# PSUM places of one bank, a fourth score bank, and the attended rows handed to ScalarE and GpSimd in an attention stage on Trainium2

## The reference, cut to what matters

```
def _L1_xattn_ref(q, k, v):              # q: normed x (4, 512, 512); k = v = ctx (4, 512, 128)
    qh = q.reshape(B, S, 8, 4, 16).transpose(0, 2, 3, 1, 4)
    kh = k.reshape(B, S, 8, 16).transpose(0, 2, 1, 3)
    vh = v.reshape(B, S, 8, 16).transpose(0, 2, 1, 3)
    scores = einsum('bkgsd,bktd->bkgst', qh, kh) / sqrt(16)
    weights = softmax(scores)
    out = einsum('bkgst,bktd->bkgsd', weights, vh)
    return out.transpose(0, 3, 1, 2, 4).reshape(B, S, E)
x = x + _L1_xattn_ref(_layernorm(x), ctx_512, ctx_512)
```

## Time and profile before

| what | value |
|---|---|
| median of three runs | 1669.87 us (1669.15 to 1671.94) |
| the profiled execution, its span | 1670.3 us |
| TensorE busy | 1567.2 us, 94% |
| VectorE busy | 948.0 us, 57% |
| ScalarE busy | 717.6 us, 43% |
| GpSimd busy | 702.1 us, 42% |

### The profile page before, as it was taken

The page is one execution under the profiler, slowest core; times in us unless marked ns, Lnnn a source line. Parts: engine busy times, 40 slices in busy tenths (PEclk is TensorE's granted clock), DMA queues, the critical chain, the costliest instruction groups (busy, mean ns, idle before and its releaser), DMA issues.

```text
span 1670.3 us, 24439 instructions
## 1 busy us (share of the span) xinstructions
PE 1567.2 (94%) x8124; PEld 1047.5 (63%) x8150; DVE 948.0 (57%) x1539; ACT 717.6 (43%) x1160; POOL 702.1 (42%) x479
## 2 busy tenths in 40 slices
PE   6869999999889999999899899999999999999998
PEld 4555657565543434434333778788788888788886
DVE  6998979796878897887885622222122222222221
ACT  5885646455547777777677211111111111111111
POOL 1124251633513125254354765670862180930064
PEclk9889999999898999999999999999999999999999
DMA  9189800000231445243430625231440140530088
GB/s 357 56 305 386 291 1 1 0 1 1 84 94 47 123 132 149 82 126 111 148 114 28 224 70 189 82 120 32 182 176 26 59 155 26 188 127 26 26 140 213
DMA packets 90944, 196.16 MB, mean 117 GB/s; under 512 B 7153, under 2 KB 9074, under 8 KB 90226
## 3 DMA queue, kind: packets, MB, share of 16 engines
q1 hardware_dynamic: 71746, 156.68, 28.2%
q0 software_dynamic: 7168, 17.04, 4.5%
q10 hardware_dynamic: 11952, 21.43, 3.9%
HBM read 113.28 MB, written 81.32 MB: 117 GB/s over the span
## 4 chain that ended last, share of the span: by engine, by line
PE 68%; DVE 16%; POOL 6%; ACT 4%; issue 3%; DMA 3%; another core or an unknown queue 0%; SPq 0%; POOLq 0%; DVEq 0%; ACTq 0%
PE psum L2929 11%; PE psum L2931 11%; PE psum L2930 11%; PE psum L2580 6%; DVE neg_max L2057 5%; PE psum L2782 5%; PE psum L2771 5%; PE psum L2744 4%; POOL expert_weight_parts L1052 3%; PE psum L2625 3%; PE psum L2595 2%; DMA w_of_even_expert<-in_L_ffn_w 2%; PE psum L2953 2%; POOL expert_weight_parts L1051 1%; DVE inner_rotated_t_second L1926 1%
## 5 line engine op out<-in xcount | busy, mean ns | idle before, releaser
L2057 DVE TENSOR_REDUCE neg_max<-psum 128x2 f32<-128x1024 f32 x248 | 291.3, 1220 | 49.5 <-PE psum L2744 48.3
L1420 ACT ACTIVATE probabilities<-psum 128x512 f32<-128x512 f32 x512 | 271.7, 601 | 85.2 <-PE psum L2771 81.3
L2199 DVE TENSOR_TENSOR expert_inner<-psum,expert_inner 128x512 f32<-128x512 f32 x78 | 53.9, 692 | 388.7 <-ACT expert_inner L1526 378.6
L2929 PE MATMUL psum<-expert_weight_parts,sorted_tokens_t_first 128*128 x624 | 250.8, 402 | 8.8 <-POOL expert_weight_parts L1052 5.1
L2930 PE MATMUL psum<-expert_weight_parts,sorted_tokens_t_first 128*128 x624 | 246.8, 396 | 0.0
L2931 PE MATMUL psum<-expert_weight_parts,sorted_tokens_t_second 128*128 x624 | 246.8, 395 | 0.0
L1526 ACT ACTIVATE expert_inner<-psum 128x512 f32<-128x512 f32 x78 | 46.7, 599 | 396.7 <-PE psum L2931 396.7
L2771 PE MATMUL psum<-query_rows,key_rows 50*128 50x512 f32 x512 | 179.3, 444 | 4.1 <-ACT probabilities L1420 3.0
L2744 PE MATMUL psum<-key_rows,query_rows 48*128 48x512 f32 x496 | 170.6, 491 | 11.7 <-DVE neg_max L2057 5.8
L2929 PEld LDWEIGHTS psum<-expert_weight_parts,sorted_tokens_t_first 128*128 128x128 f32 x624 | 117.7, 189 | 37.4 <-issue 11.1
L2782 PE MATMUL psum<-probabilities,value_and_one 128*32 128x512 f32 x1024 | 140.3, 620 | 0.8 <-ACT probabilities L1420 0.7
(11 more groups left out here) (316 smaller groups left out, 2924.3 us busy)
## 6 DMA issues: line engine op xcount, KB each, us to landing
sorted_x<-zero_rows SPq DMA_DIRECT2D x9, 3960.0 KB, 30.5
w_of_odd_expert<-in_L_ffn_w SPq DMA_DIRECT2D x8, 2048.0 KB
wo_of_expert<-in_L_ffn_wo SPq DMA_DIRECT2D x7, 2048.0 KB, 8.6
query_rows<-query_rows_of_units SPq DMA_DIRECT2D x64, 192.0 KB, 3.5
w_of_even_expert<-in_L_ffn_w SPq DMA_DIRECT2D x6, 2048.0 KB, 11.6
sorted_tokens<-sorted_x ACTq DMA_DIRECT2D x39, 264.0 KB, 2.8
sorted_y<-expert_out ACTq DMA_DIRECT2D x39, 256.0 KB
query_rows_of_units<-dims_first SPq DMA_DIRECT2D x32, 256.0 KB
```

The source lines that it names most:

```text
L1420: nc.scalar.activation(prob[t % 2][:, i * SEQ:(i + 1) * SEQ], bank[4 + n % 3], ACT.Exp, scale=HD ** -0.5).then_inc(c_e, 1)
L2057: nc.vector.tensor_reduce(of_pair[:, p, st, :], ring(("max", (m, i))).rearrange("p (h n) -> p h n", h=2), AX.X, ALU.max, negate=True).then ...
L2199: nc.vector.tensor_tensor(h, bank[2 * half + 1], h, ALU.mult).then_inc(e_h, 1)
L2929: nc.tensor.matmul(out_bank, hi[:, cols], w_r[:, bass.ds(w_at, 512)], start=start, stop=False)
```

## The change

The ring gets three places of one bank (banks 0, 1, 2), and bank 3 becomes the fourth score bank. Each maximum matmul has its own place, and VectorE reads each with a reduction of 512 columns. Score n waits for the exponential n - 4. This holds for the maxima of units 1 to 31; unit 0's are still made in pairs before the stage. The transposed attended rows are no longer read by VectorE in place: ScalarE copies them into SBUF, in step 2 between its second and third exponential, and that copy frees the place. VectorE then takes the reciprocal from SBUF after the reductions of step 2, GpSimd multiplies and adds. The last unit's rows are still normed by VectorE. The router's transposes go in four pieces of 512 columns in place of two of 1024.

```
-        place = {job: i % 2 for i, job in enumerate(jobs)}
+        place = {job: i % 3 for i, job in enumerate(jobs)}
         def ring(job):
-            return psum[:, 1024 * place[job]:1024 * place[job] + 1024]
+            return bank[place[job]]
+        def score_bank(n):
+            return bank[(4, 5, 6, 3)[n % 4]]
...
-            routing_jobs[(u_ + 1, 3)] = [("xt", (b_, 1))]
+            routing_jobs[(u_ + 1, 2)] = [("xt", (b_, 1))]
+            routing_jobs[(u_ + 1, 3)] = [("xt", (b_, 2)), ("xt", (b_, 3))]
...
-                    jobs += [("max", (u_ + 2, 2 * t_)), ("max", (u_ + 2, 2 * t_ + 1))]
+                    jobs += [("max", (u_ + 2, 4 * t_ + j)) for j in range(4)]
```

GpSimd:

```
             def add_attended(u):
                 b, j = u // KVH, u % KVH
                 pool.wait_ge(c_eo, u + 1)
+                o = att_o[:].rearrange("p (n c) -> p n c", c=32)
+                c.step(nc.gpsimd.tensor_tensor(att_n[u % 2][:].rearrange("p (n c) -> p n c", c=HD), o[:, :, 0:HD],
+                                               att_r[:].rearrange("p (n c) -> p n c", c=1).broadcast_to([P, ST * GROUP, HD]), ALU.mult))
```

ScalarE:

```
+            def attended_rows_out(u):
+                act.wait_ge(c_at, u + 1)
+                if u > 0:
+                    act.wait_ge(c_x, u)
+                nc.scalar.activation(att_o[:], ring(("attended", u)), ACT.Copy).then_inc(c_oe, 1)
+
             def attention(u):
                 for t in range(ST):
                     if there(u):
                         for i in range(4):
                             n = 16 * u + 4 * t + i
+                            if (t, i) == (2, 2) and there(u - 1):
+                                attended_rows_out(u - 1)
                             act.wait_ge(c_s, n + 1)
...
-                            nc.scalar.activation(prob[t % 2][:, i * SEQ:(i + 1) * SEQ], bank[4 + n % 3], ACT.Exp,
+                            nc.scalar.activation(prob[t % 2][:, i * SEQ:(i + 1) * SEQ], score_bank(n), ACT.Exp,
```

VectorE:

```
-                        for i in (2 * t, 2 * t + 1):
+                        for i in range(4 * t, 4 * t + 4):
...
-                    if t == 1 and there(u - 1):
-                        normed_attended(u - 1)
+                    if t == 2 and there(u) and there(u - 1):
+                        attended_reciprocal(u - 1)
+                    if t == 1 and u == UNITS:
+                        last_normed_attended()
...
+            def attended_reciprocal(u):
+                dve.wait_ge(c_oe, 2 * u + 2)
+                o = att_o[:].rearrange("p (n c) -> p n c", c=32)
+                nc.vector.reciprocal(att_r[:].rearrange("p (n c) -> p n c", c=1), o[:, :, HD:HD + 1]).then_inc(c_eo, 1)
+
+            def last_normed_attended():
+                u = UNITS - 1
                 dve.wait_ge(c_at, u + 1)
+                dve.wait_ge(c_x, u)
```

TensorE:

```
+            def maximum(m, i):
+                p, st, h = maximum_of(i)
                 job = ("max", (m, i))
+                if i == 0:
+                    pe.wait_ge(*rows_loaded(m))
+                take(job, c_red, maxima_before(m) + i + 1)
...
             def attended_transposed(u):
                 job = ("attended", u)
-                pe.wait_ge(c_oe, u + 1)
-                take(job, c_eo, u + 1)
+                pe.wait_ge(c_oe, 2 * u + 1)
+                if u < UNITS - 1:
+                    take(job, c_oe, 2 * u + 2)
+                else:
+                    take(job, c_eo, UNITS)
...
-                if n >= 3:
-                    pe.wait_ge(c_e, n - 2)
+                if n >= 4:
+                    pe.wait_ge(c_e, n - 3)
```

More of the change, by code:

```diff
@@ L545, in ring, with maxima_before, maximum_of @@
         def ring(job):
-            return psum[:, 1024 * place[job]:1024 * place[job] + 1024]
+            return bank[place[job]]
+        def score_bank(n):
+            return bank[(4, 5, 6, 3)[n % 4]]
+        def maxima_before(m):
+            return 8 + 16 * (m - 1) if m else 0
+        def maximum_of(i):
+            pair, half = i // 2, 1 - i % 2
+            return pair // ST, pair % ST, half
         def chunk_columns(b, chunk):
-            return bank[{CTX_CHUNK: 0, 0: 1, 1: 2, 2: 3, 3: 2}[chunk]] if b == 0 else ring(("chunk", (b, chunk)))[:, 0:SEQ]
+            return bank[{CTX_CHUNK: 0, 0: 1, 1: 2, 2: 3, 3: 2}[chunk]] if b == 0 else ring(("chunk", (b, chunk)))
         def second_dims(n):
@@ L2733, in chunk_transposed @@
                 last.then_inc(c_xt, 1)
-            def maximum(m, i, h, first):
-                p, st = i // ST, i % ST
+            def maximum(m, i):
+                p, st, h = maximum_of(i)
                 job = ("max", (m, i))
-                if first:
-                    if i == 0:
-                        pe.wait_ge(*rows_loaded(m))
-                    take(job, c_red, 8 * m + i + 1)
+                if i == 0:
+                    pe.wait_ge(*rows_loaded(m))
+                take(job, c_red, maxima_before(m) + i + 1)
                 rows = slice(64 * h, 64 * h + 3 * HD)
-                done = nc.tensor.matmul(ring(job)[:, h * SEQ:(h + 1) * SEQ], q_r[m % 4][rows, p * SEQ + st * P:p * SEQ + (st + 1) * P],
-                                        k_r[m % 4][rows, :], start=True, stop=True)
-                if not first:
-                    done.then_inc(c_mx, 1)
+                nc.tensor.matmul(ring(job), q_r[m % 4][rows, p * SEQ + st * P:p * SEQ + (st + 1) * P],
+                                 k_r[m % 4][rows, :], start=True, stop=True).then_inc(c_mx, 1)
             def neg_max_transposed(m):
                 job = ("negmax", m)
-                pe.wait_ge(c_red, 8 * (m + 1))
+                pe.wait_ge(c_red, maxima_before(m + 1))
                 take(job, c_nsb, m + 1)
@@ L2826, in routing_step, with batch_transposed @@
                     rank(of)
-            def batch_transposed(b, half):
-                pe.wait_ge(d_xn, b * ST + 2 * half + 2)
-                job = ("xt", (b, half))
-                take(job, d_trs, 2 * b + half + 1)
-                for st in (2 * half, 2 * half + 1):
-                    for k in range(DC):
-                        last = nc.tensor.transpose(ring(job)[:, (st % 2) * SEQ + k * P:(st % 2) * SEQ + (k + 1) * P],
-                                                   xr[b][0][:, st * WIDE + k * P:st * WIDE + (k + 1) * P], ident[:])
+            def batch_transposed(b, st):
+                pe.wait_ge(d_xn, b * ST + st + 1)
+                job = ("xt", (b, st))
+                take(job, d_trs, ST * b + st + 1)
+                for k in range(DC):
+                    last = nc.tensor.transpose(ring(job)[:, k * P:(k + 1) * P],
+                                               xr[b][0][:, st * WIDE + k * P:st * WIDE + (k + 1) * P], ident[:])
                 last.then_inc(d_tr, 1)
```

46 lines of the change are left out of this document (22 added, 24 removed).

## The result

The changed kernel takes 1730.28 us (median of 4 runs, 1721.47 to 1735.32), the kernel before 1669.76 beside it (4 runs): a recorded ratio of 1.0354, 95% interval 1.0327 to 1.0382 (the two medians alone give 1.0362). That is slower, as forecast, but 20 us above the 1710 given and 2 us beyond the end of the range (1728). The profiled execution took 1728.57 us with a span of 1726.8, 56.5 more than before.

What follows compares the result with a forecast made beforehand. Bound by the order of waits inside a step, with three engines nearly equally busy. 1.36 us in 29 units gives 39.4; - 2 + 0.5 - 1 + 3.9 = 40.8 us, so 1710 us; case range 1692 to 1724, stated range 1660 to 1728.

Steps and rivals of the forecast that it cites:

- Step 2: Third step of a unit: ScalarE's copy, behind two exponentials, delays the third maximum and `attend`; +1.1 us per unit.
- M10: Step 2's third maximum, taking the attended rows' place: forecast to start at +2.15 after the first score instead of +1.05.
- Step 1: Second step of a unit: fourth maximum waits for the first's reduction, delayed by transposed maxima; `attend` later, +0.2 us.
- The tail: End of the stage: GpSimd's queue starts 3.0 us later and unit 30's product adds 0.9; together +3.9 us.
- Reductions: VectorE: sixteen reductions of 512 columns replace eight of 1024, +0.5 us per unit; without the product, work stays about 10.4.
- the estimate of 1.25 us per unit: VectorE, from the skill's fixed instruction cost: eight more instructions cost 1.25 us per unit, perhaps 9 us more in total.
- half is regained: Rival: wait at M10 stays, but the three other steps run up to 0.33 us shorter each; 1684 us, chance 0.15.
- faster: Rival: ScalarE's copy ends by +0.7, before M10 is due, and VectorE sets the pace; 1652 us, chance 0.17.
- Steps 3 and 0: Steps without extra work: the fourth maximum's wait replaces the fourth score's bank wait; +0.03 us each, +0.06 per unit.
- The 2 us taken off for units with statistics: Taken off the 39.4 us sum, for units in which statistics make VectorE late already; 2 us.
- The clock falls: Rival: a 1.1 us stall in every unit lowers TensorE's clock, adding 1.3 us per unit; +38, 1748 us, chance 0.05.
- It costs nothing until the end of the stage: GpSimd's product: 0.74 us while nobody waits, with 2.8 us or less of work in most units; no cost before the end.

Runs made afterwards that it cites:

- e2: Changed kernel's layout alone (three one-bank places, four score banks), reciprocal and product again on VectorE straight from PSUM: 1690.54 us, 1.0101 times the kernel before.
- e7: e2 with four one-bank places for the maxima and three score banks, product on VectorE: 1658.77 us, 0.9969 times the kernel before.
- e10: Changed kernel with four unread matmuls filling TensorE's wait for the copy, run beside e9: 1712.5 us, 1.0303 times the kernel before.
- e8: e1 with `attend` moved in front of each step's fourth maximum: six runs between 1712 and 1757 us, 1.0307 times the kernel before.
- e9: The changed kernel itself, unedited, run again on the same chip as e10: 1726.72 us, 1.0351 times the kernel before.
- e1: Changed kernel with ScalarE's copy written ahead of step 2's first exponential instead of before the third: 1690.23 us, 1.0092 times the kernel before.
- e12: e7 with `attend` before the fourth score and the copy out of its bank before step 0's fourth exponential: 1651.83 us, 0.9926 times the kernel before.
- e11: Changed kernel with the copy between the first and second exponential of step 2: 1699.39 us, 1.0217 times the kernel before.
- e6: e1 with three score banks in turns and bank 3 left idle: 1691.56 us, 1.0176 times the kernel before.

## Why the prediction was right in direction and short in size

**The chain of waits held, step by step.** Step 2: copy's end forecast at +2.10 and M10 at +2.15, measured +2.10 and +2.16; `attend` forecast at +2.8, measured +2.83. Step 1: `attend` forecast 0.2 later, measured at +1.78 of its step against +1.62, 0.16 later. The tail (GpSimd's queue at the end): forecast +3.9, measured +3.3. Reductions: four in a row take 2.48, as the earlier trace rows said, and VectorE is busy for 10.65 per plain unit against 10.38, a comparison in which the product of 0.42 has left. With the product still on VectorE a plain unit keeps it busy for 11.07 (e2) or 10.90 (e7): eight more instructions cost 0.5 to 0.7, as the forecast's +0.5 said. The Trainium skill (page "VectorE: DVE Perf Modes", section "The TRN2 errata") tells of a fixed cost of about 150 cycles per instruction, and of operands in SBUF, where these lie in PSUM. By the estimate of 1.25 us per unit made from it, about half came: in a row part of the fixed cost is hidden, not all. GpSimd's product takes 0.63, and never held up the copy. The step that was argued against two rivals ("half is regained", "faster") was argued rightly: nothing was regained, a unit grew by 1.50.

**The small term that was short.** Steps 3 and 0 were given +0.03 each. In the unit shown, step 3 takes 2.74 (626.54 to 629.28) and step 0 takes 2.74 too. In the plain unit of the earlier trace rows they took 2.67 and 2.61, so together they grew by 0.20. The gate was named rightly (the fourth maximum waits for the reduction of the first), but it lies 0.1 later than the score's wait that it replaces (+1.32 against +1.18). That is the 0.14 per unit between 1.36 and 1.50. The 2 us taken off for units with statistics were wrong in sign: unit 9, of that kind, grew from 13.21 to 14.92, by 1.71. Against both, the units with router transposes grew less than counted (0.44 in three of them, 0.87 in two). At full clock the 27 units sum to 373.8 us in e10 and to 339.0 in the kernel before (350.07 less its own 11.1): +34.8, where the forecast's terms for them give 27 x 1.36 - 2 - 1 = 33.7. That these agree to 1 us is in part luck: terms that were short and terms that were long cancel. Two small slips of the working change nothing: ScalarE has 2.3 us to spare in both units of the earlier trace rows, not 1.7 to 2.3, and the upper bound of 1.7 per unit, with the other terms, leads to 1722 and not 1724.

**The step that failed** is "The clock falls" as a rival of its own, with a chance of 0.05. It was set up as another way in which it could go, with a stall that cost each unit its clock; so the sum of the likeliest case held no clock at all, although had shown that a stall of this kind can be followed by `attend` at the lower clock, and the earlier trace rows a mean clock of 0.98 over the stretch (four stretched units, as it turned out, not one). It was both at once, and in part: nine of 27 units, 16.1 us in one profile and 27.9 in another, against 11.1 in the kernel before. Where the Trainium skill's page "TensorE: Matmul & The Clock Gate" (section "A second HAM failure mode") tells of idle times between PSUM groups that make the clock swing, the traces agree for stalls of 1.20 to 1.49 us: filled with work that nobody reads, the same waits ran at 1.00. They don't show idle time as the only cause (e8's units at 0.50 had none).

A second step failed beside it: "It costs nothing until the end of the stage", of GpSimd. In unit 28 a product on VectorE lasts until GpSimd's instruction ends, 1.5 us longer than before, as shown below.

Against the forecast's 40.8 the profile's 56.5 add up like this: units 1 to 27 +34.8 by waits (33.7 forecast) and +5.0 by the clock (16.1 less 11.1; not forecast); before unit 1 +3.7 (0.5 forecast; unit 0 took 16.17 at a clock of 0.55, and 13.26 and 13.27 at 0.78 in e9 and e10, so 2.9 of this is the clock too and varies from run to run); units 28 and 29 +6.5 (2.7 forecast); the way to the power +3.3 (3.9 forecast); the rest +3.1 (none forecast). So the clock in units 0 to 27 holds some 8 of the 15.7 us that the sum missed in this profile, units 28 and 29 another 3.8.

In unit 28 (+5.8 us) the clock is not alone. The timelines of GpSimd and VectorE there:

```profile
924.76 4.54 POOL L1070 TENSOR_TENSOR expert_weight_parts<-w_of_even_expert,expert_weight_parts 128x2048 fp32r<-128x2048 f32 x1 [0.18 <-POOL expert_weight_parts L1069]
...
926.42 2.92 DVE L2182 TENSOR_TENSOR slot_picked<-logits,largest_logit 128x32 f32<-128x32 f32 x1
929.27 2.47 DVE L2082 TENSOR_REDUCE neg_max<-psum 128x1 f32<-128x512 f32 x4
```

A small product of 32 columns lasts 2.92 us, and TensorE waits. Its kind takes 0.19 elsewhere in this trace. It ends at 929.34, 0.04 us after GpSimd's splitting of expert weights (924.76 + 4.54 = 929.30), which was under way when it began. The same place in the kernel before and in e1:

```profile
877.37 4.58 POOL L1052 TENSOR_TENSOR expert_weight_parts<-w_of_even_expert,expert_weight_parts 128x2048 fp32r<-128x2048 f32 x1 [0.18 <-POOL expert_weight_parts L1051]
...
880.61 1.39 DVE L2151 TENSOR_TENSOR slot_picked<-logits,largest_logit 128x32 f32<-128x32 f32 x1
```

```profile
885.41 4.51 POOL L1070 TENSOR_TENSOR expert_weight_parts<-w_of_even_expert,expert_weight_parts 128x2048 fp32r<-128x2048 f32 x1 [0.18 <-POOL expert_weight_parts L1069]
...
885.48 4.49 DVE L2182 TENSOR_TENSOR slot_picked<-logits,largest_logit 128x32 f32<-128x32 f32 x1
```

In thirteen of the fourteen profiles this product ends 0.04 to 0.06 us after GpSimd's instruction, however long it lasts: 1.08 to 1.93 where VectorE still norms the rows (the kernel before, e2, e7, e12), 2.35 to 4.50 where GpSimd does. In the fourteenth, e8's, it begins 0.13 before GpSimd's instruction and takes 0.19, and the next product (1.51) is the one that ends so. The change set the two against each other: GpSimd's addition, which stands ahead of the splitting in its queue, now waits for the copy and the reciprocal, and starts 5.03 us after step 2's first score (922.02) where it was 0.90 (874.62). So the long instruction starts later and covers more of the product. No run moved GpSimd's queue alone.

**What stays open.** How much of the median's 60 us the clock holds: e9 and e10 say 8 to 14, with intervals that touch. Why only some stalls of 1.20 us lower it; with the copy one place earlier (e11) one unit of the 27 was stretched. How unit 28's 5.8 us divide into the product, the wait for the copy and the clock. Where the 3 us after the power come from (in e10, at the same waits, it is 6). Nor was it tried whether filling the stalls of e12 gains anything.

## What to carry to other kernels

When a buffer's release moves to another engine, it is the place in that engine's order that counts, not its load: price the copy by what is written ahead of it, one pitch (0.49 us here) for each instruction. Before a bank is given to one ring, ask which job of the other ring takes over the wait: here the fourth score's wait went, the fourth maximum's came, and the same bank on the other side made the kernel 0.3% shorter. And where the trace of before shows even one stall followed by matmuls at the lower clock, a change that adds stalls of that size gets a clock term in its sum, beside the waits and not in place of them. Last, an instruction that is handed to a queue with spare time still shifts all that stands behind it there: look for what another engine does at the new time.

## What the runs showed of the hardware that was not expected

Work that nobody reads can pay: 216 matmul records in TensorE's stalls took the mean clock of units 1 to 27 from 0.91 (e9) or 0.94 (the first profile) to 1.00 (e10) and their time from 401.7 or 389.9 to 373.8 us.

Low clock does not need stalls to last: in the profiled execution of e8, the longest of six, TensorE was busy for all of 20.94 us in units 2 and 3, at a clock of 0.50 throughout, and was back at 1.00 some 35 us later (unit 6). What let it fall and rise there, no run tells.

With reads from PSUM, instructions of VectorE overlap: one reduction of 512 columns lasts 0.68 us, four in a row 2.46 to 2.48. Halving the tile cost 0.5 us (e7) to 0.7 us (e2) of busy time per unit of sixteen.

In these profiles VectorE's small product of two operands in SBUF, begun while GpSimd's 4.5 us instruction on SBUF is under way, does not end before that one: it stretched from 0.19 us to as much as 4.50 (e6) and ended 0.04 to 0.06 us after it. VectorE's four reductions out of PSUM kept their 2.48 us beside the same instruction (e7, 865.04 to 867.52 within 864.52 to 869.10).
